# P.V of a unit of four heads: three steps on the tensor engine become one

## What is computed

```python
scores = jnp.einsum('bhqd,bhkd->bhqk', q, k) / math.sqrt(hd)
scores = jnp.where(causal, scores, -jnp.inf)
att = jax.nn.softmax(scores, axis=-1)
out = jnp.einsum('bhqk,bhkd->bhqd', att, v)
```

## Time and profile before

| | |
|---|---|
| median of 3 runs | 942.58 us (942.15 to 944.62) |
| the profiled execution: its own time | 943.2 us |
| its span, first to last instruction | 941.6 us |
| PE busy | 887.2 us (94%), 5790 matmuls |
| DVE, ACT, POOL busy | 524.5 (56%), 458.0 (49%), 497.5 us (53%) |
| share of the DMA engines | 39.6% in queue 1 |
| granted TensorE clock, mean | 0.98 of full speed |

### The profile page before, as it was taken

How to read it: one execution, slowest core, us unless ns; L and a number is a source line. 1 busy time by engine, 2 the same in 40 slices (tenths; PEclk the granted TensorE clock), 3 DMA queues, 4 the chain that set the end, 5 groups by cost and what they waited for, 6 DMA issues and landing times. The chain is left out here.

```text
span 941.6 us, 16765 instructions
## 1 busy us (share of the span) xinstructions
PE 887.2 (94%) x5790; PEld 645.2 (69%) x5790; DVE 524.5 (56%) x1543; ACT 458.0 (49%) x838; POOL 497.5 (53%) x747
## 2 busy tenths in 40 slices
PE   6778999999999899999999999999999999999887
PEld 3654655666788666677678886677667876566677
DVE  5455454756756656644576566545476474454353
ACT  2343444545646435444475555444375454344542
POOL 6834445453565534555555665455455666454343
PEclk7889999999999999999999999999999999999999
DMA  6534151523241421527172642827344463721131
GB/s 190 123 106 105 41 119 36 119 68 87 77 89 58 108 68 47 119 84 154 57 145 71 148 95 75 159 67 136 90 113 106 107 140 106 149 63 61 54 90 35
DMA packets 62146, 91.01 MB, mean 97 GB/s; under 512 B 9104, under 2 KB 31120, under 8 KB 62064
## 3 DMA queue, kind: packets, MB, share of 16 engines
q1 hardware_dynamic: 62064, 89.95, 39.6%
HBM read 77.21 MB, written 12.71 MB: 95 GB/s over the span
## 5 line engine op out<-in xcount | busy, mean ns | idle before, releaser
L921 POOL TENSOR_TENSOR w_lo<-w_raw,w_hi 128x512 fp32r<-128x512 f32 x204 | 268.3, 1320 | 84.6 <-ACT w_hi L988 80.8
L981 ACT ACTIVATE p<-s_ring 128x512 f32<-128x512 f32 x320 | 183.4, 597 | 175.2 <-PE s_ring L1381 174.5
L1213 DVE CUSTOM_DVE_ANT_0 s_ring<-s_ring,causal 128x384 f32<-128x384 f32 (+3 forms) x512 | 239.0, 515 | 48.1 <-PE s_ring L1358 47.2
L968 POOL TENSOR_SCALAR_AFFINE_SELECT p<-p 128x256 f32<-128x256 f32 (+1 forms) x320 | 121.0, 381 | 255.2 <-ACT p L981 252.8
L1245 PE MATMUL g_ring<-xt_hi,w_hi 128*128 128x512 f32 (+1 forms) x504 | 214.4, 425 | 6.8 <-DVE xt_lo L1143 3.1
L1245 PE MATMUL g_ring<-xt_lo,w_hi 128*128 128x512 f32 (+1 forms) x504 | 200.2, 397 | 0.0
L1245 PE MATMUL g_ring<-xt_hi,w_lo 128*128 128x512 f32 (+1 forms) x504 | 199.6, 396 | 0.0
L988 ACT ACTIVATE w_hi<-w_raw 128x512 fp32r<-128x512 f32 x204 | 127.6, 627 | 51.0 <-PE acc L1245 25.0
L1381 PE MATMUL s_ring<-q_op,k_op 99*128 99x384 bf16 (+3 forms) x512 | 118.8, 304 | 12.3 <-DVE maxima L1213 6.2
L1245 PE MATMUL acc<-w_hi,h_hi 128*128 128x256 f32 (+1 forms) x400 | 123.3, 308 | 4.1 <-DVE h_lo L1194 4.1
L1358 PE MATMUL s_ring<-k_op,q_op 96*128 96x384 bf16 (+3 forms) x512 | 115.8, 303 | 8.9 <-DVE maxima L1213 4.5
(11 more groups left out here) (86 smaller groups left out, 1138.9 us busy)
## 6 DMA issues: line engine op xcount, KB each, us to landing
w_raw<-weights_in SPq DMA_DIRECT2D x204, 256.0 KB, 2.7
q_op<-qk_scratch SPq DMA_DIRECT2D x96, 128.0 KB, 4.4
qk_scratch<-qk_parts SPq DMA_DIRECT2D x26, 384.0 KB, 2.6
k_op<-qk_scratch SPq DMA_DIRECT2D x48, 128.0 KB, 4.3
x<-x_in SPq DMA_DIRECT2D x8, 256.0 KB, 4.5
y_out<-x SPq DMA_DIRECT2D x8, 256.0 KB, 2.6
k_op<-qk_scratch SPq DMA_DIRECT2D x24, 64.0 KB, 3.0
bo_all<-bo_in SPq DMA_DIRECT2D x2, 256.0 KB, 5.1
```

The costliest lines, as they stand in the source:

```text
L921: pool.tensor_tensor(w_lo[:, c % SPLIT, :], w_raw[:, c % RAW, :], w_hi[:, c % SPLIT, :].bitcast(F32), ALU.subtract).then_inc(split_done, 1)
L968: pool.affine_select(out=view, in_=view, compare_op=ALU.is_ge, fill=0.0, base=0, pattern=[[0, n], [1, P]] if n == 2 else [[1, P]], channel ...
L981: act.activation(p32[:, j % PRING, :], s_ring[r % SRING][:, :], ACT.Exp, scale=SCALE).then_inc(exp_done, 1)
L1213: last = dve.tensor_tensor_reduce(out=s_ring[r % SRING][:, at:at + n], in0=s_ring[r % SRING][:, at:at + n], in1=causal[:, 512 - n:], scale ...
```

## The change

The three entries of `PV_BLOCKS` become one, in the same order of blocks (512, 384, 128, 256 columns, four heads each). There is one PV step in a unit, it waits for the mask of the tenth job, and `pv_done` counts units. In the planner the step costs 2.6 in place of three of 0.96, and its due place is 1.05. The exponential of job j waits for the PV of the unit that used the buffer. No matmul, no exponential and no transfer is added or taken away. The core of the diff:

```diff
-LAST_JOB = (3, 7, 9)
...
-PV_BLOCKS = (tuple((j, 0, j, 0) for j in range(4)),
-             tuple((j, 1, 4 + j, 0) for j in range(4)) + tuple((j, 3, 4 + j, 3 * P) for j in range(4)),
-             tuple((j, 2, 8 + j // 2, j % 2 * 2 * P) for j in range(4)))
-
-
-def pv_of_job(j):
-
-    return j // JOBS, sum(j % JOBS > last for last in LAST_JOB)
+PV_BLOCKS = (tuple((j, 0, j, 0) for j in range(4))
+             + tuple((j, 1, 4 + j, 0) for j in range(4)) + tuple((j, 3, 4 + j, 3 * P) for j in range(4))
+             + tuple((j, 2, 8 + j // 2, j % 2 * 2 * P) for j in range(4)))
...
-         "Mt": 0.17, "T": 0.24, "PV": 0.96, "otr": 0.44}
+         "Mt": 0.17, "T": 0.24, "PV": 2.6, "otr": 0.44}
...
-PV_AT = (0.55, 0.95, 1.1)
+PV_AT = 1.05
...
     def p_freed(j):
-        return at("PV", *pv_of_job(j - PRING)) if j >= PRING else 0.0
+        return at("PV", (j - PRING) // JOBS) if j >= PRING else 0.0
...
-        return max(v, at("p", JOBS * u + LAST_JOB[s]), at("oev", u - 1) if u else 0.0)
+        return max(v, at("p", JOBS * u + JOBS - 1), at("oev", u - 1) if u else 0.0)
...
                     if j >= PRING:
-                        act.wait_ge(pv_done, n_pv[pv_of_job(j - PRING)])
+                        act.wait_ge(pv_done, n_pv[(j - PRING) // JOBS])
...
-                    pe.wait_ge(mask_done, n_mask[JOBS * u + LAST_JOB[n_step]])
-                    for j, kt, job, at in PV_BLOCKS[n_step]:
+                    pe.wait_ge(mask_done, n_mask[JOBS * u + JOBS - 1])
+                    for j, kt, job, at in PV_BLOCKS:
```

More of the change, by code:

```diff
@@ L287, in v_job @@
                 end["used", c] = end["x_read", xslot] = e
-        used = at("PV", 2 * QUADS - 1, 2) if (l, b) == (1, 1) else 0.0
+        used = at("PV", 2 * QUADS - 1) if (l, b) == (1, 1) else 0.0
         for i, x in enumerate(accs):
@@ L397, in trans, with pv_ready, pv @@
         end["p", j] = place("pool", done, "mask", j, i)
-    def pv_ready(u, s):
+    def pv_ready(u):
         v = max(at("v", 0, 0), at("v", 0, 1)) if u < 2 * QUADS else at("v", *PHASES[u // QUADS])
-        return max(v, at("p", JOBS * u + LAST_JOB[s]), at("oev", u - 1) if u else 0.0)
[L403 to L406, removed]
+        return max(v, at("p", JOBS * u + JOBS - 1), at("oev", u - 1) if u else 0.0)
+    def pv(u):
+        e = end["PV", u] = pe_step(pv_ready(u), "PV", u)
+        end["oev", u] = place("act", max(e, after("otr", u - 1)), "oev", u)
     def otr_ready(u):
@@ L430, in w_v @@
     def w_v(l, b, xslot):
-        return [(2.6 if l == 0 else 5.2, lambda: NEVER if (l, b) == (1, 1) and at("PV", 2 * QUADS - 1, 2) == NEVER
+        return [(2.6 if l == 0 else 5.2, lambda: NEVER if (l, b) == (1, 1) and at("PV", 2 * QUADS - 1) == NEVER
                  else v_ready(xslot), lambda part=part: v_job(l, b, xslot, part)) for part in range(1 + l)]
@@ L538, in plan @@
                              lambda u=p, i=i: trans(u, i)) for i in range(JOBS)]
-            queues["PV"] += [(where(PV_AT[n]), lambda u=p, n=n: pv_ready(u, n), lambda u=p, n=n: pv(u, n))
-                             for n in range(3)]
+            queues["PV"].append((where(PV_AT), lambda u=p: pv_ready(u), lambda u=p: pv(u)))
             queues["O"].append((where(OTR_AT), lambda u=p: otr_ready(u), lambda u=p: otr(u)))
@@ L631, in two_layers @@
     n_mask = by(numbered(GP, "mask"), 1)
-    n_pv = by(numbered(PE, "PV"), 1, 2)
+    n_pv = by(numbered(PE, "PV"), 1)
     n_oev = by(numbered(SE, "oev"), 1)
@@ L755, in two_layers @@
         ctx_used = {i: n_g_made[ctrs[4 * i + 3][1]] for i in range(4)}
-        v_before = {(0, 0): None, (0, 1): None, (1, 0): None, (1, 1): n_pv[(2 * QUADS - 1, 2)]}
+        v_before = {(0, 0): None, (0, 1): None, (1, 0): None, (1, 1): n_pv[2 * QUADS - 1]}
         rest_before, before = {}, None
@@ L990, in _ @@
                     u = s[1]
-                    act.wait_ge(pv_done, n_pv[(u, 2)])
+                    act.wait_ge(pv_done, n_pv[u])
                     if u:
@@ L1386, in _ @@
                 elif kind == "PV":
-                    _, u, n_step = s
+                    _, u = s
                     l, b = PHASES[u // QUADS]
[L1389 to L1395, removed]
-                    pe.wait_ge(mask_done, n_mask[JOBS * u + LAST_JOB[n_step]])
-                    for j, kt, job, at in PV_BLOCKS[n_step]:
+                    if u == 0:
+                        pe.wait_ge(ones_made, 1)
+                    if u % QUADS == 0:
+                        pe.wait_ge(acc_freed, max(v_made[(0, 0)], v_made[(0, 1)]) if l == 0 else v_made[(1, b)])
+                    if u:
+                        pe.wait_ge(oev_done, n_oev[u - 1])
+                    pe.wait_ge(mask_done, n_mask[JOBS * u + JOBS - 1])
+                    for j, kt, job, at in PV_BLOCKS:
                         slot, vh = v_head(u, j)
```

## The result

The changed kernel takes 947.15 us (median of 11 runs, 945.68 to 951.28), the kernel before beside it 943.44 us (11 runs, 942.15 to 946.87). The ratio is 1.0043, 95% interval 1.003 to 1.0056: slower by 3.7 us or 0.4%, outside the range of the prediction and on the other side of its sign. The profiled execution of the changed kernel took 945.68 us, with a span of 944.1 us, 2.5 us over that of before; the two traces explain that much of the 3.7 us.

What follows compares the result with a forecast made beforehand. PE, busy 94% of the span, was taken as the bound. The terms -14.4 - 0.5 + 2.2 + 3.2 + 1.6 gave -7.9 us, so a median of 934.7 us, with a range of 927 to 943.

Steps and rivals of the forecast that it cites:

- The size of the saving: PE's PV steps: one of 2.26 us replaces three of 2.53, with two entries fewer; 0.45 us a unit, -14.4 us.
- an entry of 0.09: Ahead of each PV step on PE: 0.09 us extra; two entries fewer in a unit save 0.18 us.
- Rival 4: PV step ends: the 0.13 us may be the last matmuls' length, so only entries count; no change, 943.8; chance 0.04.
- The exit of 0.5 us: Behind PV steps with fp32r work on both sides: 0.10 us lost at 7 places before, 2 now; -0.5 us.
- The wait for the mask, +2.2: PV in units 6 and 24 waits for its last mask, uncovered, about 1.05 us each; +2.2 us.
- "Everything else ... Cost 0": DVE, ACT, POOL and SP's DMA issues run the same steps in slightly changed order; no cost.
- The T and S runs, +3.2: T and S steps on PE sharing three buffers: eight new long runs wait 0.4 us each; +3.2 us, bounds 0 and 7.6.
- A run can cost nothing more than before: T and S steps at unit 6: held step comes 1.58 us after the one at 216.77, not 2.66; PV step wholly gained.
- the prediction's first premise: Most of the kernel, PE 97% busy from 100 to 860 us: time taken from PE's list comes off the total.
- rival 3: T and S steps on `s_ring`: its three buffers become the bound, 0.44 us per new neighbour; slower, 950.9; chance 0.08.
- 359 and 403 neighbours: PE's order: pairs of neighbouring T and S steps rise from 359 to 403 with the change.
- the other terms: Besides mask and K: saving -14.4, exits -0.5, T and S runs +3.2, saved time meeting unmoved waits +1.6 us.

Runs made afterwards that it cites:

- b_merged: Kernel before, old order kept, PV's steps 0 and 1 struck out and all 16 blocks run at step 2's place: 962.89 us, ratio 1.0198.
- two_12: Kernel before with PV in two steps: step 0 stays, steps 1 and 2 become one; the planner makes a new order: 938.72 us, ratio 0.9947.
- a_s26late: Changed kernel with the first three S steps of unit 26 held until 252 T steps have run: 942.81 us, ratio 0.9993.
- a_karr: Changed kernel with the planner's arrival time of q and k made 2.5 us longer; 21 PE steps move: 942.44 us, ratio 0.9981.
- b_no0: Kernel before without PV's step 0; keys 0 to 127 used only for each head's first 128 queries, in step 1: 944.52 us, ratio 1.0002.
- b_no1: Kernel before with PV's step 1 left out (keys 128 to 255 and 384 to 511 missing): 926.26 us, ratio 0.9812.
- two_01k: Kernel before with PV steps 0 and 1 made one, step 2 alone, planner's q and k arrival 2.5 us later: 955.81 us, ratio 1.0124.
- a_warm: Changed kernel with filler matmuls, results overwritten, ahead of the mask waits of units 6 and 24 and S of unit 26: 946.90 us, ratio 1.002.
- a_both: Changed kernel with unit 26's first three S steps held back and PV of unit 6 behind two out steps: 946.48 us, ratio 1.0025.
- two_12k: Kernel before with PV step 0 alone, steps 1 and 2 made one, planner's q and k arrival 2.5 us later: 939.08 us, ratio 0.9958.

## Why the prediction was wrong

**The size of the saving was right.** 2.28 us a PV step for 2.26, an entry of 0.09, in the changed kernel, in b_merged and (1.42 us for 768 columns) in two_12. The Trainium skill's rule that changing the tiling mode drains TensorE (TensorEngine Tiling (Array Packing), Key Properties) agrees with the trace in kind; the size is the 0.22 us that rows 3 and 4 gave. Rival 4, that the step does not do what it says, is out. The exit of 0.5 us was not measured by itself.

**The wait for the mask, +2.2, was found at the right two places and sized too low.** It is 1.03 us in unit 6 (1.05 predicted), but 2.58 in unit 24, because the mask took 2.07 us there and not the 0.41 of the earlier trace rows. And the price of a wait was taken to be its length. Behind each of the two, PV runs 1.35 to 1.37 us longer at the lower clock. That makes 6.3 us, not 2.2. The prediction said of the middle that waits of about 1 us left the clock at 1.00; the one at 224.12 did not, and in the kernel before the window of 800 to 820 us (0.91) already had the clock falling behind two shorter waits.

**"Everything else ... Cost 0" failed**, and with it most of the time. Moving PV steps 0 and 1 behind the tenth T step took 2.2 us out of the stretch in which PE covers the way of K to unit 26, and the new order took some 3 us more. The waits for K rose by 5.5 us, of which one wait, from 0.83 to 4.72, makes 3.9, and the lower clock behind it costs 1.2 more. a_s26late and a_karr take these waits and the mask's down by separate edits, and gain 4.3 and 4.7 us. The prediction had read waits on `s_ring` by maxima and exponentials alone; the row of 1.9 us for K, from which the question could have been asked, was in the same view.

**The T and S runs, +3.2, came out at +2.5 in their own rows, but the argument under it was wrong.** The prediction said "A run can cost nothing more than before" and reckoned at unit 6 that the whole PV step is gained, from the distance between S and the held T step. It left out that DVE was still busy with the S step before. b_no0 is the direct test: 27.5 us of such steps removed, nothing gained. With it fails the prediction's first premise, that every tenth of a microsecond taken from PE's list is one from the time "as long as no new wait appears": in b_no0 the new waits came with the removal itself, and at unit 6 the gain was 0.34 us and not 1.08. The waits rose by only 2.5 us in the changed kernel because its planner made a new order; b_merged, without a new plan, is rival 3: predicted 950.9, and 962.89 with the old order. (The prediction's 359 and 403 neighbours count the Mt step with T and S.)

**The sum.** PE's list was to fall by 14.9 us and its busy time fell by 8.1. Of the 6.8 between, two PV steps at the lower clock are 2.7. S and T behind the K wait at 710.62 take 1.44 and 0.65 us where 0.66 and 0.22 would do, 1.2 us. And each wait lets the tail of the matmul before it count as busy (0.38 long, 0.22 from start to start); by the view of waits there are 77 and not 65, 12 x 0.16 = 1.9 us. That leaves 1.0 us, part of which may be the lower clock of 320 to 340 us. With the 10.6 us of idle time the profiled span is accounted for: 2.5 us more where 7.9 less were forecast, 10.4 us apart. K is 6.7 of them (5.5 and 1.2), the mask 4.1 (6.3 for 2.2), and the other terms nearly cancel.

**What was shown and what not.** Shown: taking step 0 away gains nothing and taking step 1 away half of its length, and most of what is not gained stands in new waits (b_no0, b_no1); one step fewer gains if step 0 stays (two_12) and loses if it goes, with the order that the planner then makes (two_01k); the K waits and the mask waits together are worth some 4.5 us in the changed kernel. Not shown: how much of the 4.5 belongs to each, as both fell in both edits; the worth of the clock at the two masks in the median (a_warm); why a_both is 3.7 us slower than a_s26late, of which the two profiles show 2.0 in waits (for `h_lo` 4.6 to 6.3 us, K 3.1 to 4.3, `m_scratch` 0 to 1.2, mask 0.9 to 0.2, maxima 13.8 to 12.4) and 3.3 in busy time; how much of the busy time that did not fall in b_no0 and b_merged is the clock; and why two_01k lies 16.7 us above two_12k in the medians, of which the two profiles show 13.0. A version with the one step and other work in step 0's place was not tried.

## What to carry to other kernels

Before counting the removal of a step on a busy engine as a gain, ask whether the next step could have run then: look at the queue of the engine that frees its buffer, not only at the distance to the step that waits. In this kernel an engine at 97% held 27 us of work that cost nothing. When steps are merged into the last of them, list every wait that the earlier ones had covered, those of transfers begun far ahead too; and merge those that stand next to each other at the end (1 and 2 here, 0.5% faster), while the one that fills a gap stays.

## What the runs showed of the hardware

- A wait on TensorE cost more than its length. Behind waits of 1.03 us (224.12) and 2.58 us (715.59) with small matmuls ahead of them, the PV step took 3.63 and 3.65 us in place of 2.28; the granted clock of 220 to 240 us was 0.91, of 700 to 720 us 0.74. With filler matmuls up to the step it took 2.27 us. In the kernel before, behind waits of 0.60 and 0.68 us with S and T steps between them, matmuls of 512 columns start 0.43 us apart (810.25 to 810.67) where 0.23 is usual. Not every such wait did this: the one of 1.01 us at 317.53 of that kernel left the granted clock of 300 to 340 us at 1.00.
- The mask of a 128x256 part, 0.41 us on POOL in the earlier trace rows, took 2.07 us at 713.37, while DVE ran three `h_lo` operations from 713.30 on. In the trace of the changed kernel 16 of 320 masks run beside `h_lo` for 0.25 us or more, and each of these took 0.52 us or more; of the other 304 one did. In the kernel before it is the same (16, each 0.53 us or more, and one other). No run moved one away from the other.
- Executions of one program differ by several us where their waits are the same in kind: 945.68 and 950.44 us in the two profiled executions of the changed kernel, with mean granted clocks of 0.973 and 0.968.
